# Local attention on one Trainium2 core: the queries' norms as a column of the mask-and-maximum instruction

## What is computed

```python
x = x + _L0_attn_a_ref(_layernorm(x), ...)   # a state-space layer (mamba)
x = x + _L0_ffn_ref(_layernorm(x), ...)      # local transformer, first time
x = x + _L0_attn_b_ref(_layernorm(x), ...)   # dense attention
x = x + _L0_ffn_ref(_layernorm(x), ...)      # local transformer, second time
x = x + _L1_attn_a_ref(_layernorm(x), ...)   # linear attention
x = x + _L1_ffn_ref(_layernorm(x), ...)
x = x + _L1_attn_b_ref(_layernorm(x), ...)
x = x + _L1_ffn_ref(_layernorm(x), ...)
```

```python
def attn_layer(x, Wqkv, qs, ksc, Wo):
    q, k, v = jnp.split(x @ Wqkv, 3, -1)          # 16 heads of 64
    q = l2norm(q) * qs;  k = l2norm(k) * ksc      # t / max(|t|, 1e-12), per token and head
    q = q * cos * scale + rotate_half(q) * sin * scale
    k = k * cos * inv + rotate_half(k) * sin * inv
    sim = jnp.einsum('bhwie,bhwje->bhwij', bq, bk2) * QK_SCALE   # windows of 32, and the window before
    attn = jax.nn.softmax(jnp.where(mask, -max, sim), -1)
    return (attn @ bv2) @ Wo
for i in range(DEPTH):
    x = attn_layer(shift_tokens(x), ...) + x
    x = ffn_layer(shift_tokens(x), ...) + x       # layer norm, a * gelu(gate), W2
```

## Time and profile before

| | us |
|---|---|
| median of 3 runs (lowest, highest) | 4189.5 (4188.85, 4190.77) |
| the profiled execution, its own time | 4191.06 |
| its span, first to last instruction | 4189.2 |
| TensorE busy (share of the span) | 3839.1 (92%) |
| VectorE busy | 3525.8 (84%) |
| GpSimd busy | 3391.1 (81%) |
| ScalarE busy | 3337.6 (80%) |

### The profile page before, as it was taken

The page is one execution under the profiler, slowest core; times in us unless marked ns, Lnnn a source line. Parts: engine busy times, 40 slices in busy tenths (PEclk is TensorE's granted clock), DMA queues, the critical chain, the costliest instruction groups (busy, mean ns, idle before and its releaser), DMA issues. The chain is left out here.

```text
span 4189.2 us, 141892 instructions
## 1 busy us (share of the span) xinstructions
PE 3839.1 (92%) x52653; PEld 2317.7 (55%) x52653; DVE 3525.8 (84%) x11433; ACT 3337.6 (80%) x10657; POOL 3391.1 (81%) x4093
## 2 busy tenths in 40 slices
PE   6888789999999999999767999999999999996686
PEld 2333356666666666666453666666666666663464
DVE  6999889899899899899476899899899899974646
ACT  6888589999999999999514999999999999983122
POOL 3999798998998998999296999999999999871324
PEclk8999999999999999999898999999999999997888
DMA  1000111111111111011002111111111111110000
GB/s 29 1 1 1 47 27 31 43 35 36 43 32 49 30 39 44 25 35 33 12 0 63 25 28 52 28 43 40 30 43 37 43 30 38 31 25 3 6 3 10
DMA packets 78611, 122.77 MB, mean 29 GB/s; under 512 B 26024, under 2 KB 47204, under 8 KB 77924
## 3 DMA queue, kind: packets, MB, share of 16 engines
q1 hardware_dynamic: 77924, 113.71, 10.4%
HBM read 35.56 MB, written 1.05 MB: 9 GB/s over the span
## 5 line engine op out<-in xcount | busy, mean ns | idle before, releaser
L1397 ACT ACTIVATE local_pr<-local_tb,local_nmax 128x96 f32<-128x96 f32 x3072 | 1003.5, 368 | 179.1 <-DVE local_nmax L1533 172.2
L1108 POOL TENSOR_TENSOR local_qk<-local_qk,local_rb 128x512 f32<-128x512 f32 x768 | 975.0, 1281 | 107.9 <-DVE local_rb L1517 107.2
L1208 PE MATMUL local_pj<-local_wqkv,local_xs 128*64 128x512 f32 x3072 | 811.5, 607 | 27.1 <-DVE local_rb L1517 12.8
L1114 POOL TENSOR_TENSOR local_qk<-local_qk,local_rinv 128x512 f32<-128x512 f32 x768 | 791.7, 1047 | 7.5
L1397 ACT ACTIVATION_READ_ACCUMULATOR local_pr<-local_tb,local_nmax 128x1 f32 x3072 | 719.4, 234 | 0.0
L1533 DVE CUSTOM_DVE_ANT_0 local_tb<-local_tb,local_mask 128x96 f32<-128x96 f32 x3072 | 680.5, 291 | 5.7 <-PE local_tb L1233 5.7
L1524 DVE TENSOR_REDUCE local_ss<-local_sq 128x8 f32<-128x512 f32 x768 | 521.6, 680 | 183.3 <-ACT local_sq L1380 180.3
L1135 POOL TENSOR_TENSOR local_pr<-local_pr,local_rsum 128x384 f32<-128x384 f32 x768 | 624.3, 831 | 29.3 <-DVE local_rsum L1539 29.3
L1514 DVE TENSOR_TENSOR local_qk<-local_pj,local_rope 128x512 f32<-128x512 f32 x768 | 516.6, 673 | 56.0 <-ACT local_sq L1380 44.7
L1380 ACT ACTIVATE local_sq<-local_pj 128x512 f32<-128x512 f32 x768 | 499.2, 650 | 48.7 <-PE local_pj L1208 43.0
L1517 DVE TENSOR_TENSOR local_rb<-local_pj,local_rope 128x512 f32<-128x512 f32 x768 | 522.6, 680 | 0.0
(11 more groups left out here) (450 smaller groups left out, 7370.2 us busy)
## 6 DMA issues: line engine op xcount, KB each, us to landing
local_v<-local_v SPq DMA_DIRECT2D x288, 256.0 KB, 3.8
local_wqkv<-L_ffn_Wqkv_dram SPq DMA_DIRECT2D x72, 256.0 KB, 2.8
local_wo<-L_ffn_Wo_dram SPq DMA_DIRECT2D x12, 512.0 KB, 4.2
local_w<-L_ffn_W_dram SPq DMA_DIRECT2D x12, 341.0 KB, 3.0
mamba_parts<-mamba_in_low SPq DMA_DIRECT2D x24, 64.0 KB, 2.0
...
```

The lines of the kernel that those rows point to most:

```text
L1108: nc.gpsimd.tensor_tensor(qk[:, u, :], qk[:, u, :], rb[:, u % 2, :], ALU.add).then_inc(s["summed"], 1)
L1114: nc.gpsimd.tensor_tensor(heads8(qk[:, u, :]), heads8(qk[:, u, :]), r, ALU.mult).then_inc(s["scaled"], 1)
L1208: ins = nc.tensor.matmul(bank[own, :], xs[:, par, u // 4 * P + own.start:u // 4 * P + own.stop], wqkv[:, dep % 2, u % 4 * BANK:(u % 4 + 1) ...
L1397: ins = nc.scalar.activation(pr[:, (NU * c + k) % PR_RING, i, WIN:WIN + KW], scores[:, i * KW:(i + 1) * KW], ACT.Exp, scale=-1.0, bias=nma ...
```

## The change

In the local transformer, GpSimd's `scale` runs for the four key units only. The queries stay unscaled; their inverse norms, with a minus sign, are left in `rinv`, and `maxima` passes the column of the head in question, one number per partition, as the factor in place of the constant -1.0. `rinv` is doubled (one buffer per parity of the sequence), the root's ninth step is split in two so that queries get the sign, `maxima` waits for the root once per sequence, and the query couples of `turn_qk` wait for `add_parts` rather than `scale`. The diagonals move from ScalarE's two instructions to one 128x256 product on GpSimd. All orders of the local pipeline are written anew: the two rings and the lists of all five engines.

In `normalise` the dense and linear attention's weights can be turned and copied while the variance's root is worked out (class `Weights`), with 3 `warm` matmuls instead of 8, and ScalarE copies the second half of the centred stream after the turned root. In linear attention beta is loaded first, and the steps that depend on it stand earlier.

```diff
     if step == 8:
         return nc.gpsimd.tensor_tensor(y[0], t[0], x, ALU.mult)
-    if step == 9:
-        return nc.gpsimd.tensor_scalar(t[0], y[0], -0.5, 1.5, ALU.mult, ALU.add)
+    if step in (9, 10):
+        sign = (-1.0, 1.0)[step - 9]
+        of = lambda r: r.rearrange("p (t w c) -> p t w c", t=2, w=2)[:, :, step - 9, :]
+        return nc.gpsimd.tensor_scalar(of(t[0]), of(y[0]), -0.5 * sign, 1.5 * sign, ALU.mult, ALU.add)
     return nc.gpsimd.tensor_tensor(y[1], t[0], t[1], ALU.mult)
...
-            warm(nc, net, p_idle, 8)
+            if weights:
+                weights.turn(pe, p_weights)
+            warm(nc, net, p_idle, 3 if weights else 8)
             pe.wait_ge(roots, 1 + ROOT_STEPS)
             nc.tensor.transpose(p_rootT, root[:, :], net.ident[:, :]).then_inc(turned, 1)
             pe.wait_ge(copied, 1)
+            if weights:
+                pe.wait_ge(weights.ready, 1)
...
-PAIRS_OF_BANKS = [("probs", 5, 1), ("qk", 4, 2), ("score", 4, 0), ("probs", 5, 2), ("probs", 5, 3), ("qk", 4, 3),
-         ("probs", 4, 0), ("score", 4, 1), ("score", 4, 2), ("score", 4, 3), ("qk", 3, 0), ("qk", 3, 1)]
-PROJECTIONS = [("rotated", 3, 2), ("v_ready", 4, 2), ("v_ready", 4, 3), ("rotated", 3, 3), ("rotated", 3, 4), ("rotated", 3, 5),
-         ("rotated", 3, 6), ("rotated", 3, 7), ("v_ready", 3, 0), ("v_ready", 3, 1), ("rotated", 2, 0), ("rotated", 2, 1)]
+PAIRS_OF_BANKS = [("qk", 4, 1), ("probs", 5, 1), ("score", 4, 0), ("qk", 4, 2), ("probs", 5, 2), ("qk", 4, 3),
+         ("probs", 5, 3), ("probs", 4, 0), ("score", 4, 1), ("score", 4, 2), ("score", 4, 3), ("qk", 3, 0)]
+PROJECTIONS = [("rotated", 3, 1), ("rotated", 3, 2), ("v_ready", 4, 1), ("rotated", 3, 3), ("rotated", 3, 4), ("rotated", 3, 5),
+         ("rotated", 3, 6), ("rotated", 3, 7), ("v_ready", 4, 2), ("v_ready", 4, 3), ("v_ready", 3, 0), ("rotated", 2, 0)]
...
-                r = view(rinv[:, u * 8:(u + 1) * 8], [[1, 8], [0, DH]])
+                r = view(rinv[:, par, u * 8:(u + 1) * 8], [[1, 8], [0, DH]])
                 nc.gpsimd.tensor_tensor(heads8(qk[:, u, :]), heads8(qk[:, u, :]), r, ALU.mult).then_inc(s["scaled"], 1)
 
             def root(a, par, step):
 
-                x, y, t = ssc[:, :], (root0[:, :], rinv[:, :]), [r[:, :] for r in rt]
+                x, y, t = ssc[:, :], (root0[:, :], rinv[:, par, :]), [r[:, :] for r in rt]
                 if step == 0:
                     pool.wait_ge(s["summed_sq"], QK_UNITS * a + QK_UNITS)
-                    need(pool, s["scaled"], QK_UNITS * a)
+                    need(pool, s["scaled"], K_UNITS * a)
+                    need(pool, s["maxed"], NU * (a - 1))
...
+            def spread_std(e, par, _):
+                pool.wait_ge(s["std_ready"], e + 1)
+                need(pool, s["spread"], e)
+                nc.gpsimd.tensor_tensor(diag[:, :, :], view(net.ident[:, 0:1], [[0, 2], [1, P]]), view(deviation[:, 0:1], [[1, 2], [0, P]]),
+                                        ALU.mult).then_inc(s["diag_ready"], 1)
...
-                pe.wait_ge(s["scaled"], QK_UNITS * b + 2 * j + 2)
+                if j % 2:
+                    pe.wait_ge(s["scaled"], K_UNITS * b + j + 1)
+                else:
+                    pe.wait_ge(s["summed"], QK_UNITS * b + 2 * j + 2)
...
+                if k == 0:
+                    dve.wait_ge(s["root_steps"], ROOT_ALL * c + ROOT_ALL)
+                t, half = couple(k // 2)
                 for i in range(4):
-                    at = scores[:, i * KW:(i + 1) * KW]
-                    ins = nc.vector.tensor_tensor_reduce(at, at, mask[:, k // 4, :], -1.0, 3.0e38, ALU.add, ALU.min, nmax[:, k, i:i + 1])
+                    at, head = scores[:, i * KW:(i + 1) * KW], 8 * (4 * t + half) + 2 * i + k % 2
+                    ins = nc.vector.tensor_tensor_reduce(at, at, mask[:, k // 4, :], rinv[:, par, head:head + 1], 3.0e38, ALU.add, ALU.min,
+                                                         nmax[:, k, i:i + 1])
...
                 run(add_eps, 6, 0)
-                run(sum_squares, 3, 1)
                 run(copy_o, 5, 0)
-                run(rotate, 3, 2)
-                run(maxima, 4, 0)
+                run(recip, 5, 3)
                 run(maxima, 4, 1)
+                run(rotate, 3, 3)
                 run(affine, 6, 0)
-                run(shift_in, 2, 0)
-                run(sum_squares, 3, 2)
-                run(rotate, 3, 3)
+                run(sum_squares, 3, 3)
+                run(rotate, 3, 4)
                 run(recip, 4, 0)
                 run(copy_o, 5, 1)
-                run(sum_squares, 3, 3)
-                run(rotate, 3, 4)
                 run(sum_squares, 3, 4)
-                run(copy_o, 5, 2)
+                run(rotate, 3, 5)
                 run(sum_squares, 3, 5)
-                run(rotate, 3, 5)
                 run(rotate, 3, 6)
                 run(sum_squares, 3, 6)
-                run(gate, 6, 0)
+                run(copy_o, 5, 2)
                 run(sum_squares, 3, 7)
                 run(rotate, 3, 7)
+                run(gate, 6, 0)
                 run(maxima, 4, 2)
+                run(maxima, 4, 3)
                 run(gate, 6, 1)
                 run(gate, 6, 2)
-                run(maxima, 4, 3)
                 run(maxima, 4, 4)
+                run(shift_in, 2, 0)
+                run(maxima, 4, 5)
                 run(residual2, 6, 0)
-                run(maxima, 4, 5)
                 run(copy_o, 5, 3)
+                run(maxima, 4, 6)
                 run(recip, 4, 1)
-                run(sum_squares, 2, 0)
-                run(maxima, 4, 6)
                 run(maxima, 4, 7)
-                run(residual1, 5, 0)
                 run(recip, 4, 2)
                 run(rotate, 2, 0)
-                run(recip, 4, 3)
+                run(sum_squares, 2, 0)
                 run(rotate, 2, 1)
+                run(sum_squares, 2, 1)
+                run(residual1, 5, 0)
+                run(rotate, 2, 2)
+                run(sum_squares, 2, 2)
+                run(maxima, 3, 0)
...
+    def turn(self, pe, bank):
+        pe.wait_ge(self.loaded, 16 * 4)
+        for i in range(4):
+            ins = self.nc.tensor.transpose(bank[:, i * C:(i + 1) * C], self.raw[:, i, :], self.ident[:, :])
+        ins.then_inc(self.turned, 1)
+
+    def keep(self, act, bank):
+        if self.first:
+            self.first(act)
+        act.wait_ge(self.turned, 1)
+        self.nc.scalar.activation(self.kept[:, :, :].rearrange("p i c -> p (i c)"), bank, ACT.Copy).then_inc(self.ready, 1)
...
+                beta = d[p_ + "beta"]
+                sp.dma_start(cols[:, 4:5], bass.AP(beta.tensor, beta.offset, [[1, NH], [0, HD], [1, 1]])).then_inc(beta_in, 16)
+                weights.load(sp, [d[f"{p_}W{name}"] for name in "qkvo"])
```

226 lines of the change are left out of this document (108 added, 118 removed).

## The result

The changed kernel takes 4154.0 us (median of 4 runs, 4149.4 to 4155.7) against 4189.2 before: ratio 0.9914, 95% interval 0.9903 to 0.9926. It is 35 us faster, where I had forecast 46 slower. The profiled execution took 4153.05 with a span of 4151.3, 37.9 under the span of before.

| stretch | before | after | difference |
|---|---|---|---|
| start to local0's first projection | 495.9 | 494.4 | -1.4 |
| the two fills (first projection to first `down`) | 113.2 + 111.7 | 105.1 + 106.6 | -13.2 |
| 2 x 40 regular intervals | 80 x 31.433 | 80 x 31.422 | -0.8 |
| 2 x 4 last full intervals | 8 x 31.96 | 8 x 31.42 | -4.3 |
| the two drains (last three intervals) | 74.8 + 75.6 | 70.8 + 70.9 | -8.8 |

What follows compares the result with a forecast made beforehand. TensorE's own instruction stream, 31.43 us a sequence, was taken as the bound, with a nearly equal loop through VectorE and ScalarE. Longer intervals +49 and weights -3 made +46: 4237 profiled, 4235 as median; range 4178 to 4252, likeliest case 4198 to 4247.

Steps and rivals of the forecast that it cites:

- The column's price: VectorE's 32 maxima per sequence: each 0.058 us longer with a column as factor, 20 of them one behind another.
- The loop: Local stages, `variance` to `turn_qk(3,0)` through VectorE and ScalarE: 20.57 plus 20 column prices, 21.73, against TensorE's 21.1.
- The 0.18 of the earlier trace: TensorE's idling in the old kernel at `turn_qk(3,0)`, released by ScalarE's exponentials; said to cost next to nothing.
- TensorE's floor: TensorE's own work per sequence in the new order: 31.50 us, some 0.07 more for an added group of turns and scores.
- The third rival: Shape changes on TensorE cost less than counted, floor 31.35 and column free: 4176; chance 0.06.
- GpSimd and ScalarE "worth nothing by themselves; they only give room for the new orders": GpSimd loses 4.2 us of products per sequence, ScalarE two diagonals of 0.5 us; neither is the bound, so no gain.
- The 0.6 of slack: GpSimd's new diagonals, between `variance` and `spread`: 0.6 us to spare before TensorE would wait at `spread`.
- The rival that makes ScalarE the bound by its share: ScalarE, 470.74 of 500 busy, sets the period; without the diagonals it falls to 30.85: -52, 4135; chance 0.04.
- Fill and drain 0 within 4: Ends of the local stages: a sequence's way through the order stays as long to half a microsecond, 0 within 4 us.
- The last four stay: Last four full intervals of a local stage, already longer because the residual's second add runs on VectorE: no change.
- The first rival: The column costs nothing to speak of, under 0.026; TensorE's 31.50 rules: 4190 profiled, 4188 as median; chance 0.30.
- The weights: Dense and linear attention's weights turned inside the normalisation: -3 us together (0 to -6).

Runs made afterwards that it cites:

- const_factor: The changed kernel with the constant -1.0 as the maxima's factor instead of the column, so the queries' norms are left out: 4151.4 us, ratio 0.9909.
- second profiled execution: The changed kernel, nothing altered, profiled again: regular interval 31.42, drains of 144.6 instead of 141.6.
- residual_ahead: The changed kernel with one step moved, VectorE's second residual ahead of maxima(4,5) again instead of behind it: 4215.2 us, ratio 1.0056.
- weights_only: The kernel before with only the change's part outside the local stages, weights turned inside the normalisation: 4187.8 us, ratio 0.9996.

## Why the prediction was wrong, point by point

- **The column's price** is the term that was mis-sized, and the largest: it made +49, and the period gave -0.8. It is 0.032 an instruction in a run of four, and 0.61 / 20 = 0.030 on the loop, where I took 0.058 from the earlier trace rows; that lies between the two cases to which I had given a chance, 0.026 and less or 0.037 and more. The first of a run does pay what the pairs of the earlier trace rows pay (0.060, against 0.050 to 0.063); those behind an accumulator's read pay 0.023. The rows are mean durations, too, and not distances between starts: for the first pair those differ by 0.063 as well (0.401 and 0.338), for the second no run shows it. I had named the read as what could hide a fetch, and then took the full price because the instructions follow each other without a gap. Three of four stand behind such a read, and with the constant these took 0.042 longer than the first (0.215 against 0.173), with the column only 0.005. That the fetch hides under the read fits this; it wasn't isolated.
- **The loop was right** in its place (the turn behind score(4,3), released by ScalarE's exponentials), and nearly in its length: 21.06 in the trace, beside 20.99 of TensorE's own (the same two starts in const_factor). Lengthened by 0.40 it cost 0.50, shortened by 0.88, and by the whole price of the column, it gave 0.06 each time. My sum without the column was 0.12 too long, so the break-even is (20.99 - 20.45) / 20 = 0.027, not far from my 0.026, and TensorE's 21.1 was 0.1 too high as well. With the right price my own formula gives 31.5, within 0.1 of the measured 31.42.
- **What bounds the kernel.** I read the earlier trace rows as proof that no block waits. That was too strong: the score ahead of the turn of the next sequence's queries takes 0.88 there, at 1116.02, and 0.82 where the loop is shortened. The old period moved from 31.433 to 31.477 between two kernels with the same local code, and a column put 0.43 on it at once: the old loops had next to no slack. Such waits are the same in every round, so equal intervals don't rule them out, and a busy time of 500.00 doesn't show them. The 0.18 of the earlier trace rows, at this very turn, was a better sign than the 500.00 of the earlier trace rows.
- **TensorE's floor** was put at 31.50, 0.07 above the old period as if that held no wait; it is 31.353. The third rival named 31.35, but as a mere assumption. The drain at a change of tiling mode, for which I named the Trainium skill (TensorEngine Tiling (Array Packing), Key Properties), is there in the rows: 0.96 for a projection ahead of a change and 0.91 behind one, 0.86 elsewhere. Whether the seventh group lengthened the stream is open: no run shows the old order without its waits.
- **GpSimd and ScalarE "worth nothing by themselves; they only give room for the new orders"** holds for the period: in the old orders four products fewer changed nothing (31.867 both times; for the diagonals no run shows it there), and the new orders need the room, 1.15 a sequence for the products and 0.35 for the diagonals. What I left out is that without this room the new orders lose. The "nothing" failed in the fill, where the products alone are worth 5.9 us. The 0.6 of slack that I counted ahead of `spread` holds only with the queries' scaling gone; with it TensorE stands there, the one place that I had named. The rival that makes ScalarE the bound by its share is still not borne out: the period did not fall to its 30.85, and ScalarE is about as busy after as before.
- **"Fill and drain 0 within 4"** is the other step that failed: -13.2 and -8.8, in the second profiled execution -12.6 and -5.8. I had compared how long one sequence's way through TensorE's order is; but in the fill TensorE waits for GpSimd's products, which the trace of before showed (9.3 us in one row that I did not ask for), and in the drain for what an order puts between `variance` and `spread`, and in both the granted clock was higher in the changed kernel. **"The last four stay"** failed by -4.3, although the first rival had it (-4): `residual2` ahead of maxima(4,5) makes them, as residual_ahead shows (32.68 against 31.92).
- **The first rival** came nearest in its mechanism, a period that hardly moves, and its 4188 was 34 too high, for it lacked the ends too. Fills -13.2, drains -8.8 and a clock at the normalisations that happened to be higher, -5.5, make 27.5 of it; the period, which it put at +6 and which gave -0.8, makes most of the rest.
- **The weights**, -3: -3.8 in the rows, and too little to be seen in the time of weights_only.
